# Attention by head pairs, with the reciprocals of the softmax sums carried through the transpose

## The reference, cut to what matters

```python
h = h + attn(layernorm(h))
# attn: n = 375
xn = (x - mu) / sqrt(var + 1e-05) * gamma + beta
q, k, v = (causal 3-tap depthwise convolution of w @ xn) per head, q * 64 ** -0.5
sim = einsum('bhid,bhjd->bhij', q, k) - slope[h] * abs(i - j)   # causal mask above it
out = einsum('bhij,bhjd->bhid', softmax(sim), v) @ wout.T
```

## Time and profile before

| | |
|---|---|
| median of 3 runs | 1566.08 us (1565.75 to 1567.41) |
| the profiled execution | 1568.55 us, its span 1566.8 us |
| busy: PE, DVE, ACT, POOL | 1354.8, 952.7, 671.4, 264.4 us |
| mean granted TensorE clock | 0.924 |

### The profile page before, as it was taken

One profiled execution on the slowest core, in us unless ns is written; L12 is line 12 of the kernel. 1 busy time (PEld: TensorE's weight loads), 2 busy tenths in 40 slices (PEclk: granted clock), 3 DMA queues, 4 the chain that ended last, 5 costly groups with the idle time before them and its releaser, 6 DMA issues. The chain is left out here.

```text
span 1566.8 us, 26688 instructions
## 1 busy us (share of the span) xinstructions
PE 1354.8 (86%) x7905; PEld 1089.1 (70%) x7905; DVE 952.7 (61%) x3107; ACT 671.4 (43%) x1759; POOL 264.4 (17%) x262
## 2 busy tenths in 40 slices
PE   6999999999369999989999899999997896466663
PEld 5999999999356777766767667677665685355553
DVE  3433434334569898879878798788874566621211
ACT  2334334333235655656546565456653341021211
POOL 6000000000010001001110000100000400178885
PEclk9999999999679999999999999999998898687877
DMA  4000000000100000000000000000000112044542
GB/s 106 17 15 20 20 10 20 20 10 20 35 11 10 2 22 23 22 21 17 10 17 21 21 20 10 14 21 12 12 12 20 28 34 60 6 79 81 97 82 39
DMA packets 93851, 43.86 MB, mean 28 GB/s; under 512 B 31295, under 2 KB 90088, under 8 KB 93752
## 3 DMA queue, kind: packets, MB, share of 16 engines
q1 hardware_dynamic: 69960, 36.25, 8.5%
q0 software_dynamic: 23808, 6.69, 3.3%
HBM read 29.52 MB, written 10.18 MB: 25 GB/s over the span
## 5 line engine op out<-in xcount | busy, mean ns | idle before, releaser
L783 ACT ACTIVATE P<-P,nmax 125x375 f32<-125x375 f32 (+2 forms) x384 | 189.1, 494 | 292.1 <-DVE nmax L923 291.9
L287 PE MATMUL bank<-h1hl,W2hl 128*128 128x376 f32 x1536 | 278.0, 336 | 2.9 <-DVE h1hl L402 2.9
L287 PEld LDWEIGHTS bank<-h1hl,W2hl 128*128 128x128 f32 x1536 | 264.0, 189 | 3.1 <-DVE h1hl L402 3.1
L624 PE MATMUL bank<-QK 64*125 64x375 f32 (+2 forms) x768 | 197.8, 391 | 13.4 <-DVE nmax L923 13.4
L624 PEld LDWEIGHTS bank<-QK 64*125 64x125 f32 x768 | 112.8, 185 | 75.8 <-DVE nmax L923 25.0
L364 ACT ACTIVATE h<-bank,b2c 128x375 f32<-128x375 f32 x128 | 73.5, 574 | 207.3 <-PE bank L287 207.3
L923 DVE CUSTOM_DVE_ANT_0 P<-bank,nbias 125x375 f32<-125x375 f32 (+2 forms) x384 | 139.7, 413 | 2.6 <-PE bank L624 2.5
L1569 ACT ACTIVATE hE<-bank,EB 128x375 f32<-128x375 f32 x64 | 36.7, 573 | 199.0 <-PE bank L1544 196.4
L680 PE MATMUL bank<-WVT,xnThl 128*125 128x512 f32 x432 | 115.7, 413 | 3.0 <-DVE QK L972 3.0
L913 DVE TENSOR_SCALAR P<-P,prec 125x375 f32<-125x375 f32 (+2 forms) x384 | 111.9, 347 | 4.5
L865 POOL TENSOR_SCALAR lnve<-lnmv 125x3 f32<-125x3 f32 x32 | 10.1, 315 | 575.6 <-DVE lnmv L891 575.6
(11 more groups left out here) (196 smaller groups left out, 2363.4 us busy)
## 6 DMA issues: line engine op xcount, KB each, us to landing
X<-in_x_dram SPq DMA_DIRECT2D x34, 375.0 KB
EW<-in_L_ffn_w_dram SPq DMA_DIRECT2D x32, 256.0 KB
token_table<-row SPq DMA_DIRECT2D x16, 210.9 KB
tTall<-tT SPq DMA_DIRECT2D x16, 187.5 KB, 2.3
out_dram<-oS SPq DMA_DIRECT2D x16, 187.5 KB
tTall<-in_L_tok_W_dram SPq DMA_DIRECT2D x1, 1024.0 KB, 7.1
EB<-in_L_ffn_b_dram SPq DMA_DIRECT2D x16, 62.5 KB
tok<-token_table,ids POOLq DMA_INDIRECT x48
```

The costliest lines, as they stand in the source:

```text
L287: last = nc.tensor.matmul(bank[4 + m % 2][:, :NE], W2hl[:, a, k, m * 128:(m + 1) * 128], h1hl[:, p, b, k], start=(k == 0 and n == 0), stop ...
L624: last = nc.tensor.matmul(bS[unit][:PT_, at:at + w], QK[r:r + DH, 0, c, i * PT_:(i + 1) * PT_], QK[r:r + DH, 1, c, :w], start=True, stop=True)
L783: nc.scalar.activation(P[:, h % 4, SEG[q]:SEG[q] + w], P[:, h % 4, SEG[q]:SEG[q] + w], ACT.Exp, bias=nmax[:, h % 4, q:q + 1], scale=-1.0, ...
```

## The change

- A pair of heads takes two steps. `scores(b, c, part)`: part 0 is tile 2 of both heads, part 1 tiles 1 and 0 of both. The two heads alternate, one on rows 0 to 63, the other on 64 to 127, and each head has a PSUM bank of its own. The maxima of a part are one group on DVE (`biased_max`), the exps of a part one group on ACT.
- P isn't normalised. The row sums of a pair are spread over 64 columns a head and their reciprocals taken (`prec`, 125 x 3 x 2 x 64). PE transposes prec too, three transposes a pair, tile i behind a group of the transposes of P, into columns 375 to 499 of a bank bT. The copy to PT takes them along. DVE multiplies the pair's output in bO with them on the way to OT, in place of ACT's copy.
- Transposes of P take 128 columns in place of 125, with three zero columns behind P.
- ACT copies all of bT to PT; DVE copied a quarter of it.
- The pair's transposes come one pair behind the scores and `attend` two pairs behind.
- The layer norm of the tower and that of the attention are one: var is multiplied with (1 + eps) and eps squared added before the root. The two normalisations of h (for attention and for the gate) are applied by GpSimd, each in two tensor-tensor passes over 125 x 3 x 128.
- The cell maxima (L951) are taken by GpSimd, into two buffers.

The core of the diff:

```diff
-            SEG = (0, N, N + PT_)
-            ORDER = (2, 0, 1)
-            LN = 9
+            SEG = (N, N + PT_, 0)
+            LN = 7
+            PW = 2 * N + 3
+            TW = N + PT_
...
-            psum_ = sb_("psum_", [PT_, 4, NT])
-            prec = sb_("prec", [PT_, 4, NT])
-            PT = sb_("PT", [PT_, 4, 2 * N])
+            psum_ = sb_("psum_", [PT_, 2, NT, 2])
+            prec = sb_("prec", [PT_, 2, NT, 2, DH])
+            PT = sb_("PT", [128, 2, 4, TW])
...
+            PARTS = ((2,), (1, 0))
+            ORDER = ((2, 0), (2, 1)), ((1, 0), (0, 0), (1, 1), (0, 1))
...
+                def scores(b, c, part):
+                    n = 4 * b + c
                     pe.wait_ge(s_qk, 8 * b + 2 * c + 2)
+                    wait(pe, s_s, 6 * n + 2 * part)
+                    for i in PARTS[part]:
+                        w, at = (i + 1) * PT_, 0 if i else 2 * PT_
+                        for q in range(2):
+                            r = DH * q
+                            last = nc.tensor.matmul(bS[q][:PT_, at:at + w],
                                                     QK[r:r + DH, 0, c, i * PT_:(i + 1) * PT_],
                                                     QK[r:r + DH, 1, c, :w], start=True, stop=True)
+                    last.then_inc(s_sp, 1)
...
+                def transpose_probs(b, c, q):
+                    n, r = 4 * b + c, c % 2
+                    if q == 0:
+                        pe.wait_ge(s_ex, 6 * n + 6)
+                    for half, blocks in enumerate((((0, 0), (1, 0), (2, 0)), ((1, 1), (2, 1), (2, 2)))):
+                        wait(pe, (s_pt0, s_pt1)[half], 2 * n + q)
+                        for k, (i, j) in enumerate(blocks):
+                            f = SEG[i] + j * PT_
+                            last = nc.tensor.transpose(bT[half][:, k * PT_:(k + 1) * PT_],
+                                                       P[:, 2 * r + q, f:f + 128], ident[:PT_, :PT_])
+                        i = 2 * q + half - 1
+                        if i >= 0:
+                            if i == 0:
+                                pe.wait_ge(s_rc, n + 1)
+                            last = nc.tensor.transpose(bT[half][:, N:TW],
+                                                       prec[:, r, i].rearrange("p q d -> p (q d)"),
+                                                       ident[:PT_, :PT_])
+                        last.then_inc(s_tp, 1)
...
+                        if valid(b):
+                            scores(b, c, part)
                         if h == 0 and valid(b):
                             project_qk(b, 3, u)
...
                         if p in (2, 4, 6) and valid(b + 1):
                             project_qk(b + 1, p // 2 - 1, v_)
+                        m, d = pair_before(b, c, 1)
+                        if valid(m):
+                            transpose_probs(m, d, part)
+                        m, d = pair_before(b, c, 2)
+                        if part == 0 and valid(m):
+                            attend(m, d, u if c >= 2 else v_)
...
+                def copy_probs(b, c, q):
+                    n, r = 4 * b + c, c % 2
+                    wait(act, s_o, n - 1)
+                    for half, w in enumerate((TW if q else N, TW)):
+                        act.wait_ge(s_tp, 4 * n + 2 * q + half + 1)
+                        nc.scalar.copy(PT[:, r, 2 * q + half, 0:w], bT[half][:, :w]
+                                       ).then_inc((s_pt0, s_pt1)[half], 1)
...
+                def ln_apply(dst, m, mv, r, s, n):
+                    nc.gpsimd.tensor_tensor(dst[:, :, 0:C], Hall[:, m], mv[:, :, 0:1].broadcast_to([PT_, NT, C]),
+                                            ALU.subtract).then_inc(s, 1)
+                    pool.wait_ge(s, n + 3)
+                    nc.gpsimd.tensor_tensor(dst[:, :, 0:C], dst[:, :, 0:C],
+                                            r[:, :, None].broadcast_to([PT_, NT, C]), ALU.mult).then_inc(s, 1)
...
+                        if h >= 2 and valid(b + 3):
+                            m, k = b + 3, h - 2
+                            wait_apart(pool, s_csb, m + 1, s_on[1])
+                            wait_apart(pool, s_ov, 6 * m + k - 1, s_on[1])
+                            nc.gpsimd.tensor_scalar(cellmax[:, k % 2], grid0[:], csb[:, TT_ + k:TT_ + k + 1], None,
+                                                    ALU.max).then_inc(s_cm, 1)
...
+                        m, d = pair_before(b, c, 2)
+                        if part == 1 and valid(m):
+                            n = 4 * m + d
+                            dve.wait_ge(s_pv, n + 1)
+                            wait(dve, s_wo, m)
+                            nc.vector.tensor_tensor(OT[:, d].rearrange("p (t i) -> p t i", i=PT_),
+                                                    bO[:, :N].rearrange("p (t i) -> p t i", i=PT_),
+                                                    PT[:, d % 2, 1:4, N:TW], ALU.mult).then_inc(s_o, 1)
                         if valid(b):
+                            biased_max(b, c, part)
+                        m, d = pair_before(b, c, 1)
+                        if part == 0 and valid(m):
+                            n = 4 * m + d
+                            dve.wait_ge(s_ex, 6 * n + 6)
+                            nc.vector.reciprocal(prec[:, d % 2], psum_[:, d % 2, :, :, None].broadcast_to(
+                                [PT_, NT, 2, DH])).then_inc(s_rc, 1)
```

More of the change, by code:

```diff
@@ L612, in _, with pair_before @@
                 sp.wait_ge(s_tts, 16 * B)
+            def pair_before(b, c, back):
+                return b + (c - back) // 4, (c - back) % 4
+            PARTS = ((2,), (1, 0))
+            ORDER = ((2, 0), (2, 1)), ((1, 0), (0, 0), (1, 1), (0, 1))
             @block.tensor
             def _(pe):
-                def scores(b, h):
-                    c, r = h // 2, DH * (h % 2)
+                def scores(b, c, part):
+                    n = 4 * b + c
                     pe.wait_ge(s_qk, 8 * b + 2 * c + 2)
[L619 to L624, removed]
+                    wait(pe, s_s, 6 * n + 2 * part)
[4 more added lines that the diff above has]
+                            last = nc.tensor.matmul(bS[q][:PT_, at:at + w],
@@ L645, in attend @@
                 def attend(b, c, u):
-                    pe.wait_ge(s_pt0, 8 * b + 2 * c + 2)
-                    pe.wait_ge(s_pt1, 8 * b + 2 * c + 2)
+                    n, r = 4 * b + c, c % 2
+                    pe.wait_ge(s_pt0, 2 * n + 2)
+                    pe.wait_ge(s_pt1, 2 * n + 2)
                     pe.wait_ge(s_v, 3 * b + 3)
[L649 to L654, removed]
+                    wait(pe, s_o, n)
@@ new lines, in attend @@
+                    for j in range(NT):
+                        half, at, w = min(j, 1), (j // 2) * 2 * PT_, N - j * PT_
+                        for q in range(2):
+                            last = nc.tensor.matmul(bO[DH * q:DH * (q + 1), j * PT_:N],
+                                                    V[:, u, j, (2 * c + q) * DH:(2 * c + q + 1) * DH],
+                                                    PT[:PT_, r, 2 * q + half, at:at + w],
+                                                    start=(j == 0), stop=(j == NT - 1))
@@ L703, in body @@
                     for h in range(HEADS):
+                        c, part = h // 2, h % 2
                         if valid(b):
[L705 to L709, removed]
+                            scores(b, c, part)
                         if h == 0 and valid(b):
@@ L775, in _, with exps @@
             def _(act):
+                def exps(b, c, part):
+                    n, r = 4 * b + c, c % 2
+                    for k, (i, q) in enumerate(ORDER[part]):
+                        w = (i + 1) * PT_
+                        act.wait_ge(s_s, 6 * n + 2 * part + k + 1)
+                        nc.scalar.activation(P[:, 2 * r + q, SEG[i]:SEG[i] + w], P[:, 2 * r + q, SEG[i]:SEG[i] + w],
+                                             ACT.Exp, bias=nmax[:, 2 * r + q, i:i + 1], scale=-1.0,
+                                             accum_out=psum_[:, r, i, q:q + 1]).then_inc(s_ex, 1)
@@ L776, in body @@
                 def body(b, u):
                     for h in range(HEADS):
-                        if valid(b):
[L779 to L811, removed]
+                        c, part = h // 2, h % 2
+                        p = projection_step(b, h)
+                        m, d = (b, 3) if p == 0 else (b + 1, p // 2 - 1)
@@ L812, in body @@
+                        if h not in (1, 2) and valid(m):
+                            act.wait_ge(s_ov, 6 * m + k + 1)
+                            wait(act, s_ein, m)
+                            nc.scalar.activation(Wt[:, k], overlap[:, k % 2], ACT.Relu).then_inc(s_wt, 1)
                         if p in (3, 5, 7) and valid(b + 1):
@@ L891, in ln_stats, with biased_max @@
                         nc.vector.bn_aggr(mv[:, t], stat[:, t]).then_inc(s, 1)
```

(30 more changed lines are left out.)

167 lines of the change are left out of this document (51 added, 116 removed).

## The result

The changed kernel takes 1665.38 us (median of 4, 1662.25 to 1667.33) against 1565.91: a ratio of 1.0631, 95% interval 1.0611 to 1.0651. It is 99 us slower. The profiled execution took 1667.33, its span is 1664.9, the mean granted clock 0.898 (0.924 before).

What follows compares the result with a forecast made beforehand. PE was taken to bound the kernel, almost without gaps. Profiled 1568.5 us + 141 (round trips over sixteen batches) + 30 (clock) = 1739.5, given as 1737 for the median; own range 1670 to 1800, stated range 1505 to 1825.

Steps and rivals of the forecast that it cites:

- the mechanism named: Attention stage: PE's transposes wait for DVE's wide reciprocal, behind maxima that wait for PE's scores; 54.9 us a batch against 46.1.
- The forecast's own range: Whole kernel: 1670 to 1800 us, from a reciprocal of 3.0 to 4.0 us and a clock cost of 0 to 58.
- the streamed reciprocal: Rival: DVE's reciprocal of 384 elements costs 0.56 us like a copy, giving 1514 us; chance 0.25.
- PE was the bound, and the scores of a pair would take what one head's do: Attention: PE has 45.1 of 46.1 us work a batch; a pair's scores take 1.46 us, saving 5.8 a batch.
- the rival of the row halves: PE's scores: row halves don't overlap; 1608 us with a streamed reciprocal (chance 0.05), 1831 with the slow one (0.04).
- The reciprocal costs 3.6 us: DVE, four times a batch: 384 elements at 9 ns each plus 0.15 us give 3.6 us.
- The reciprocal lies on a round trip: Every pair: PE stands still about 3.1 us for DVE's reciprocal, which lies behind the maxima of the new scores.
- Pooling takes 5.33 us: PE, once a batch at step 1: pooling priced at 5.33 us from a trace row, ending at 13.5 in its pair.
- The clock costs 30 us: Attention stage: PE's stalls lower the granted clock, costing 0 to 58 us, taken as 30.
- GpSimd's and ACT's parts are hidden: GpSimd's maxima and applies, some 12 us more in 55, and ACT's wider copies, at most 2.4 us, add no time.
- The first rival: DVE's wide reciprocal streams in 0.56 us; 42.9 us a batch and 1514 us in all, faster; chance 0.25.
- The signs: Expected in the profile: clock below 0.95, pooled-token copy every 55 to 57 us, DVE busy about 40 of 50.

Runs made afterwards that it cites:

- apart: Against the kernel with six-sum reciprocal and copy before the maxima (1489.7 us): heads' score products no longer alternate, a one-column product between them; 1585.71 us.
- widths: Same 1489.7 us kernel (six-sum reciprocal and copy before the maxima), plus reciprocals and copies of 1 to 375 columns once at the stage's start; 1498.61 us, one run.
- first: Changed kernel, wide reciprocal kept but placed before the maxima of the new scores in DVE's program; 1556.52 us.
- behind: Changed kernel plus a second, unused reciprocal of 375 columns on DVE behind the overlap of every even step; 1682.87 us, one run.
- filler: Changed kernel plus two unused 375-column products on PE before the second half of each pair's transposes; 1618.92 us.
- cell_dve: Against the kernel with six-sum reciprocal and copy before the maxima (1489.7 us): cell maxima moved from GpSimd back to DVE; 1489.90 us.
- apply_dve: Against the kernel with six-sum reciprocal and copy before the maxima (1489.7 us): both layer-norm applies moved from GpSimd back to DVE; 1483.76 us.
- both_dve: Against the kernel with six-sum reciprocal and copy before the maxima (1489.7 us): cell maxima and both applies back on DVE; 1487.68 us.
- narrow_copy: Changed kernel with the reciprocal taken of a pair's six sums, then spread over 64 columns by a DVE copy; 1509.64 us.

## Why the prediction was right, and where its terms were off

It said 1737 us and slower; it is 1665.4 and slower, by the mechanism named. The base of the sum is the profiled time: 1739.5 forecast, 1667.3 measured. The forecast's own range, 1670 to 1800, does not hold 1665.4. The stated one does, only because it was stretched down to 1505 for the streamed reciprocal, which didn't come. So the sign and the mechanism were right, and the size was about 70 us too high.

- *PE was the bound, and the scores of a pair would take what one head's do.* They take 1.66 us a pair, not 1.46. In apart even one head's part takes 0.82 us alone, so the 0.2 come with the cut into two parts. That is 0.2 x 64 = 13 us more than forecast. That the halves overlap at all is shown by apart. The Trainium skill's "TensorEngine Tiling (Array Packing)" (Key Properties), by which the rival of the row halves fell away, agrees with these traces (0.83 us for two heads, 0.82 for one).
- *The reciprocal costs 3.6 us.* This is the term of the sum that was most mis-sized: "At 9, 384 elements take 0.15 + 383 x 0.009 = 3.6 us" measured 2.55. 1.05 us x 64 = 67 us too much. The sign of the argument stood (the streamed 0.56 was the rival), but its base was two differences of some 20 ns, and widths shows that a copy has the same difference: that 9 ns lay as near to the true 6.26 as it did was luck. The 8 cycles that I read from the Trainium skill's "VectorE: DVE Perf Modes" (First, the fixed hardware budget) would give 3.35; the measurement has 6.26 ns, which would be 6 cycles of 0.96 GHz, and decides.
- *The reciprocal lies on a round trip.* Right: first (same work, 109 us less) and behind (160 us of work more, 17 us more) show it from both sides. The waits of the profile were those named, 1.4 to 2.0 us a pair outside the jump where I had 3.1. Of the difference, 1.05 is the reciprocal's.
- *Pooling takes 5.33 us.* It was read at 892.63 us, just behind the loop's jump, where the granted clock from 885 to 900 us is 0.89. In the batch before, at 843.23, the same 36 records take 4.10 and not 5.49. In the changed kernel pooling takes 3.93 from start to start at the full clock (940.24 to 944.17). A row read at the low clock, and the clock then charged once more: 1.4 x 16 = 22 us too much.
- *The clock costs 30 us.* 1739.5 - 67 - 22 + 13 = 1663.5, against 1667.3, so the term comes out near 34 by the sum; filler says it is 46 or more. If both hold, some 12 us of the chain, such as the hand-overs, were put too long; they were not taken apart.
- *GpSimd's and ACT's parts are hidden.* Right for the maxima (cell_dve: same) and, to some 6 us that stay open, for the applies (apply_dve 6 us less, both_dve 2). What I named as the danger, that GpSimd holds up a pass of DVE, did happen to the copies of narrow_copy, but not to the wide reciprocal, 2548 ns in the mean. ACT's part was tested only within the whole.
- *The first rival*, a reciprocal as short as a copy, would have given 1514. narrow_copy made just that change, 0.49 us from start to start, and gave 1509.6. The 4 us between them are partly luck, since the 13 and the 22 us from above stand against each other. But the whole outcome of the change did hang on this one instruction. The reciprocal, its copy and their place made 176 us of difference on a few lines (1665.4 to 1489.7).
- *The signs.* A clock of 0.90 came as named (below 0.95), 54.6 us a batch nearly (55 to 57); DVE was busy 34 of 50 us, not about 40.

## What to carry to other kernels

Take a reciprocal before its result is spread, not after: its time goes with the columns, and six columns and a copy do what 384 columns did. Where two engines hand work to each other once a round, ask what of it can be done while waiting for the other; the wide reciprocal cost 156 us against the narrow one behind that wait and 67 in front of it (1556.5 against 1489.7). And when durations are read from a trace to price something, look at the granted clock of that very stretch first.

## What the runs showed of the hardware

- VectorE's reciprocal of fp32 takes 6.26 ns a column (2501 ns for 375, 753 for 96), a copy from SBUF some 0.5 (354 and 210 for the same). With six columns the reciprocal is 183 to 185 ns.
- PE stalls of 1.4 to 2.0 us, four in a batch of 54.6 us (every eighth, at the loop's jump, 5.3 to 5.9), went with a mean clock of 0.90; with two products of no use in each the clock was 0.97 and the kernel 46 us faster.
- A DVE copy of 125x384 from SBUF to SBUF takes 0.36 us alone and up to 0.94 while GpSimd does a tensor-tensor pass over 125x384 in SBUF (narrow_copy).
- Two fp32 products on the two row halves take as long as one (0.83 us against 0.82).
